# A routed two-block network on one core: marks and low halves on GpSimd, and another order around the routing

## What is computed

```python
x = _rmsnorm(hidden_states, ln_weight).reshape(-1, H)
logits = x @ router_weight
probs = jax.nn.softmax(logits, axis=-1)
top_vals, top_idx = jax.lax.top_k(probs, TOP_K)          # 4 of 16
aff = jnp.zeros((T, E)).at[jnp.arange(T)[:, None], top_idx].set(top_vals)
gu = jnp.einsum('th,ehi->eti', x, gate_up_proj)
gate, up = jnp.split(gu, 2, axis=-1)
expert_out = jnp.einsum('eti,eih->eth', jax.nn.silu(gate) * up, down_proj)
routed = jnp.einsum('te,eth->th', aff, expert_out)
shared = (jax.nn.silu(x @ shared_gate_w) * (x @ shared_up_w)) @ shared_down_w
return routed + shared
```

## Time and profile before

| | us |
|---|---|
| median of three runs | 1042.9 (1041.71 to 1045.14) |
| profiled execution: span from first to last instruction | 1041.2 |
| PE busy | 943.6 (91%) |
| DVE busy | 652.2 (63%) |
| ACT busy | 539.3 (52%) |
| POOL busy | 143.6 (14%) |

### The profile page before, as it was taken

The page is one execution under the profiler, slowest core; times in us unless marked ns, Lnnn a source line. Parts: engine busy times, 40 slices in busy tenths (PEclk is TensorE's granted clock), DMA queues, the critical chain, the costliest instruction groups (busy, mean ns, idle before and its releaser), DMA issues. The chain is left out here.

```text
span 1041.2 us, 21125 instructions
## 1 busy us (share of the span) xinstructions
PE 943.6 (91%) x7748; PEld 616.8 (59%) x7749; DVE 652.2 (63%) x1272; ACT 539.3 (52%) x857; POOL 143.6 (14%) x166
## 2 busy tenths in 40 slices
PE   5898988499999999999999999999999959975796
PEld 4444534267766666766776767677664438862453
DVE  5376786265666556566556665665666776677773
ACT  3655687155665545555556655654654213234674
POOL 0000000202102101210111210112016810002000
PEclk9989988799999999999999999999999979997999
DMA  8770633657885765776668776857887510000001
GB/s 290 247 234 1 232 131 132 199 159 240 263 263 182 244 194 189 242 260 195 217 213 255 228 252 211 252 201 233 260 240 230 162 47 1 1 0 1 1 21 61
DMA packets 164882, 181.76 MB, mean 175 GB/s; under 512 B 54609, under 2 KB 132433, under 8 KB 164850
## 3 DMA queue, kind: packets, MB, share of 16 engines
q1 hardware_dynamic: 152338, 147.35, 43.5%
q0 software_dynamic: 9808, 32.12, 9.7%
q10 hardware_dynamic: 2704, 1.87, 0.6%
HBM read 155.09 MB, written 14.68 MB: 163 GB/s over the span
## 5 line engine op out<-in xcount | busy, mean ns | idle before, releaser
L1083 DVE SCALAR_TENSOR_TENSOR w_lo<-raw_first,w_hi 128x1024 f16<-128x1024 f32 x144 | 172.6, 1223 | 82.4 <-ACT w_hi L577 80.6
L844 PE MATMUL pa<-x,w_hi 128*128 128x256 f16 (+2 forms) x576 | 172.5, 299 | 22.7 <-issue 13.3
L845 PE MATMUL pa<-x,w_hi 128*128 128x256 f16 (+2 forms) x576 | 172.3, 299 | 0.0
L846 PE MATMUL pa<-x,w_lo 128*128 128x256 f16 (+2 forms) x576 | 172.3, 299 | 0.0
L844 PE MATMUL pb<-x,w_hi 128*128 128x256 f16 (+2 forms) x576 | 170.9, 297 | 0.0
L845 PE MATMUL pb<-x,w_hi 128*128 128x256 f16 (+2 forms) x576 | 170.7, 296 | 0.0
L846 PE MATMUL pb<-x,w_lo 128*128 128x256 f16 (+2 forms) x576 | 170.6, 296 | 0.0
L577 ACT ACTIVATE w_hi<-raw_first 128x1024 f16<-128x1024 f32 x144 | 147.8, 1049 | 0.0
L585 ACT CAST early<-between 128x320 f16<-128x320 f32 (+1 forms) x144 | 68.4, 475 | 147.0 <-DVE between L1088 143.9
L1083 DVE SCALAR_TENSOR_TENSOR w_lo<-raw_last,w_hi 128x1024 f16<-128x1024 f32 x72 | 88.2, 1225 | 82.8 <-ACT w_hi L577 82.8
L1093 DVE TENSOR_TENSOR early<-between,early 128x320 f16<-128x320 f32 (+1 forms) x144 | 74.1, 515 | 74.8 <-ACT early L585 74.7
(11 more groups left out here) (272 smaller groups left out, 1621.2 us busy)
## 6 DMA issues: line engine op xcount, KB each, us to landing
raw_first<-in_gate_up SPq DMA_DIRECT2D x96, 512.0 KB, 4.8
raw_last<-in_gate_up SPq DMA_DIRECT2D x32, 512.0 KB
raw_first<-in_down SPq DMA_DIRECT2D x32, 512.0 KB, 4.3
raw_last<-in_down SPq DMA_DIRECT2D x32, 512.0 KB
chunks<-in_f SPq DMA_DIRECT2D x16, 704.0 KB, 5.9
slot_y<-chunks POOLq DMA_DIRECT2D x16, 512.0 KB, 3.2
chunks<-in_f SPq DMA_DIRECT2D x6, 768.0 KB, 4.6
raw_first<-in_sgate SPq DMA_DIRECT2D x6, 512.0 KB, 6.4
```

The costliest lines, as they stand in the source:

```text
L844: T.matmul(out, hi_a, hi_b, start=first, stop=False, **flags)
L845: T.matmul(out, hi_a, lo_b, start=False, stop=False, **flags)
L846: return T.matmul(out, lo_a, hi_b, start=False, stop=last, **flags)
L1083: V.scalar_tensor_tensor(w_lo[:, j % RING, c], raw[j % RING][:, c], W_SCALE, w_hi[:, j % RING, c], ALU.mult, ALU.subtract).then_inc(split_ ...
```

## The change

- POOL makes the tokens' low halves (`z_low` is gone from DVE's list and is POOL's first step for each tile), and the second half of the marks (`mark_places(nc.gpsimd, 1)`), behind the token stores. A new semaphore `found` releases it. `sum_lists` waits for one count from each engine.
- DVE's order changes: `hidden` of steps 4, 5, 6 moves ahead of `number`, `place` and the marks; the two low halves of piece 4 go ahead of `find_places`; the cast of `lists` goes ahead of the next unit's low halves. `hidden` in unit 0 waits explicitly for the `hidden_low` two steps earlier.
- ACT's order in unit 0 changes to match: `hi` before `make_ternary`, and `hidden_high` of steps 5 to 7 later.
- The first gather takes its numbers from `lists` directly, without the copy.
- `rows_in` becomes three semaphores: SP issues each turn as soon as its own gather has landed.
- PE reads `narrow` and branches first, and waits for `turned_in` inside either branch.

The diff, cut to its core (the semaphores' declarations and the two `tensor_copy`/`link` lines of `find_places` are left out):

```diff
+        def mark_places(engine, part):
+            for i in range(part * MARK, (part + 1) * MARK):
+                engine.tensor_scalar(at_row[:, i, :], place16[:, 0:P], at_f[:, 0, i:i + 1], None, ALU.is_equal)
+                ins = engine.tensor_scalar(at_col[:, i, :], place16[:, :], at_f[:, 1, i:i + 1],
+                                           token_ids[:, i // TOPK:i // TOPK + 1], ALU.is_equal, ALU.mult)
+            return ins
...
-                    sp.wait_ge(rows_in, U * (16 * len(ROUTED)))
-                    sp.nop(nofuse=True)
                     for j, w in enumerate(ROUTED):
+                        sp.wait_ge(rows_in[j], U * 16)
+                        sp.nop(nofuse=True)
                         turn_rows(j, rows16[0:w, j, :], w)
...
             for t in range(NT):
+                pool.wait_ge(z_hi_ready, t + 1)
+                nc.gpsimd.tensor_tensor(z16[:, t % Z_RING, 1, :], rows[:, t, :], z16[:, t % Z_RING, 0, :],
+                                        ALU.subtract).then_inc(z_ready, 1)
                 pool.wait_ge(z_ready, t + 1)
                 pool.dma_start(io["tokens"][t * P:(t + 1) * P, :],
...
+            pool.wait_ge(found, 1)
+            mark_places(nc.gpsimd, 1).then_inc(placed[1], 1)
...
             pool.wait_ge(listed, 1)
-            gather(0)
+            gather_rows(lists)
...
-                pe.wait_ge(placed, MARKS)
+                pe.wait_ge(placed[0], 1)
+                pe.wait_ge(placed[1], 1)
...
-                pe.wait_ge(turned_in, (u + 1) * (16 * len(ROUTED)))
                 few = pe.value_load(narrow[0:1, bass.ds(u, 1)], min_val=0, max_val=1)
                 with pe.If(few > 0):
+                    pe.wait_ge(turned_in, (u + 1) * (16 * len(ROUTED)))
+                    pe.nop(nofuse=True)
                     unit(u + 1, tiles_of(NARROW))
                 with pe.Else():
+                    pe.wait_ge(turned_in, (u + 1) * (16 * len(ROUTED)))
+                    pe.nop(nofuse=True)
                     unit(u + 1, ROUTED)
...
             lo(0, 3, 1)
+            hidden(0, 4, HALF, first_unit=True)
             number()
-            hidden(0, 4, HALF)
+            hidden_low(0, 4, HALF)
+            hidden(0, 5, HALF, first_unit=True)
             place()
-            hidden_low(0, 4, HALF)
-            z_low(6)
-            z_low(7)
             lo(0, 4, 0)
+            lo(0, 4, 1)
             find_places()
-            hidden(0, 5, HALF)
+            hidden(0, 6, HALF, first_unit=True)
+            hidden_low(0, 5, HALF)
             mark(0)
-            hidden_low(0, 5, HALF)
-            lo(0, 4, 1)
-            hidden(0, 6, HALF)
-            mark(1)
+            hidden(0, 7, HALF, first_unit=True)
             hidden_low(0, 6, HALF)
             lo(0, 5, 0)
-            hidden(0, 7, HALF)
             hidden_low(0, 7, HALF)
             lo(0, 5, 1)
-            lo(1, 0, 0)
-            lo(1, 0, 1)
             dve.wait_ge(list_summed, 1)
             V.tensor_copy(lists[:, :], list_ps).then_inc(listed, 1)
-            for j, half in HALVES[2:AHEAD]:
+            for j, half in HALVES[0:AHEAD]:
                 lo(1, j, half)
```

More of the change, by code:

```diff
@@ L290, in attention_and_experts @@
         listed = sem("listed")
-        placed = sem("placed")
+        found = sem("found")
+        placed = [sem("placed_dve"), sem("placed_pool")]
         list_summed = sem("list_summed")
         ids_ready = sem("ids_ready")
-        rows_in = sem("rows_in")
+        rows_in = [sem(f"rows_in{j}") for j in range(UNIT_COLS)]
         x_hi_ready = sem("x_hi_ready")
@@ L475, in _ @@
             pool.wait_ge(listed, 1)
-            gather(0)
+            gather_rows(lists)
             n = rounds_of(pool)
             with pool.Fori(0, n * EXPERTS) as u:
-                gather(u + 1)
+                gather_next(u)
                 store(u)
-            pool.wait_ge(rows_in, n * (EXPERTS * 48) + 48)
-            pool.nop(nofuse=True)
+            for j in range(UNIT_COLS):
+                pool.wait_ge(rows_in[j], n * (EXPERTS * 16) + 16)
+                pool.nop(nofuse=True)
             with pool.If(n < 2):
@@ L713, in _ @@
             silu(0, 5, HALF)
+            hi(0, 4, 1)
             make_ternary(6)
+            silu(0, 6, HALF)
             hidden_high(0, 5, HALF)
-            hi(0, 4, 1)
-            silu(0, 6, HALF)
+            hi(0, 5, 0)
             make_ternary(7)
+            silu(0, 7, HALF)
+            hi(0, 5, 1)
             hidden_high(0, 6, HALF)
-            hi(0, 5, 0)
-            silu(0, 7, HALF)
+            hidden_high(0, 7, HALF)
             make_ternary(8)
-            hidden_high(0, 7, HALF)
-            hi(0, 5, 1)
             make_ternary(9)
@@ L1084, in lo, with hidden @@
                                        ALU.mult, ALU.subtract).then_inc(split_ready, 1)
-            def hidden(U, m, n):
+            def hidden(U, m, n, first_unit=False):
                 dve.wait_ge(silu_ready, U * FH + m + 1)
+                if first_unit and m >= 2:
+                    dve.wait_ge(h_ready, m - 1)
                 V.scalar_tensor_tensor(hid[:, m % 2, 0:n], up_ps[m % 2][:, 0:n], 1.0 / W_SCALE, gated[:, m % 2, 0:n],
@@ L1094, in hidden_low @@
                                 ALU.subtract).then_inc(h_ready, 1)
-            def z_low(t):
-                dve.wait_ge(z_hi_ready, t + 1)
-                V.tensor_tensor(z16[:, t % Z_RING, 1, :], rows[:, t, :], z16[:, t % Z_RING, 0, :],
-                                ALU.subtract).then_inc(z_ready, 1)
             def choose():
@@ L1180, in find_places @@
                 link(V.tensor_scalar(at_int[:, 1, :], at_int[:, 1, :], P.bit_length() - 1, None, ALU.logical_shift_right))
-                link(V.tensor_copy(at_f[:, :, :], at_int[:, :, :]))
+                V.tensor_copy(at_f[:, :, :], at_int[:, :, :]).then_inc(found, 1)
+                dve.wait_ge(found, 1)
             def mark(part):
-                for i in range(part * MARK, (part + 1) * MARK):
-                    V.tensor_scalar(at_row[:, i, :], place16[:, 0:P], at_f[:, 0, i:i + 1], None, ALU.is_equal)
-                    ins = V.tensor_scalar(at_col[:, i, :], place16[:, :], at_f[:, 1, i:i + 1],
-                                          token_ids[:, i // TOPK:i // TOPK + 1], ALU.is_equal, ALU.mult)
-                ins.then_inc(placed, 1)
+                mark_places(V, part).then_inc(placed[0], 1)
             def add_shared():
@@ L1281, in _ @@
             lo(0, 1, 1)
-            hidden(0, 0, HALF)
-            z_low(0)
+            hidden(0, 0, HALF, first_unit=True)
             hidden_low(0, 0, HALF)
-            z_low(1)
             lo(0, 2, 0)
-            hidden(0, 1, HALF)
-            z_low(2)
+            hidden(0, 1, HALF, first_unit=True)
             hidden_low(0, 1, HALF)
-            z_low(3)
             lo(0, 2, 1)
-            hidden(0, 2, HALF)
+            hidden(0, 2, HALF, first_unit=True)
             choose()
```

20 lines of the change are left out of this document (10 added, 10 removed).

## The result

The changed kernel takes 1046.7 us (median of 20 runs, 1042.0 to 1050.1) against 1042.4 before (20 runs): a ratio of 1.0044, with a 95% interval of 1.0029 to 1.0058. That is 4.6 us slower, 3.0 to 6.0; I had forecast 16 us faster. Of the two terms one came as forecast and the other with the opposite sign and a larger size. Of the later run e5, one execution in six took 2856 us; its median is that of the other five.

What follows compares the result with a forecast made beforehand. PE bounds the kernel from 241 us on; the change can pay only between 109 and 200, in PE's waits and half-clock stretches. Gains of 5.4 + 10.8 = 16.2 us give 1026.7 us, range 1023 to 1030 (chance 0.43).

Steps and rivals of the forecast that it cites:

- Term 2: From E to the first routed matmul: earlier cast, split turns and early branch cut 23.85 us to 13.05, gaining 10.8.
- E: Start of the second `down` half behind the sum on PE: 175.78 us before, forecast at 170.4.
- Term 1: Unit 0: reordered DVE work and shared marks remove PE's waits, so E comes 5.4 us earlier.
- I take 0.70 a pair, near the rows of like width: GpSimd's half of the marks: 16 pairs at 0.70 us each, 11.2 us, plus 2.4 for disturbance.
- POOL idled 32.02 us there, which hides them: Tokens' low halves on POOL: eight subtractions at 0.93 us each, 15 us in all if doubled, hidden by POOL's idle time.
- the dear end, 1.41: Rival: GpSimd no quicker with narrow operations, 1.41 us per pair of marks, gain 5.7, 1037.2 us; chance 0.08.
- the slower case: Rival: GpSimd's pair dearer through fp16 and two scalars; above 1.71 us a pair slower than before, 1055.5 at 2.5; chance 0.06.
- The halves that take turns: Rival: DVE and GpSimd block each other for whole mark operations, both done after 17.65 us, 1030.8 us; chance 0.15.
- The branch's cost: Rival: PE's early branch does not help, code fetch paid again behind the rows, 2.6 us less gain, 1029.3; chance 0.08.

Runs made afterwards that it cites:

- e5: Changed kernel with GpSimd making 7 of 32 groups of marks and `hidden` 7 moved ahead of DVE's marks: 1029.4 us.
- e7: e6 with the token low halves of tiles 6 and 7 moved behind the marks on DVE: 1029.7 us.
- e8: Kernel before with 18 scalar operations, nine forms, added on GpSimd ahead of all other work to price them: 1045.8 us, one run.
- e11: e9 with PE waiting for the turned rows ahead of the load and the branch: 1034.3 us.
- e13: Changed kernel with DVE's tail (from `hidden_low` 6) waiting for GpSimd's marks: 1044.5 us.
- e3: Changed kernel with marks split unevenly, 6 of 32 groups on GpSimd and 26 on DVE: 1034.6 us.
- e1: Changed kernel with all marks on DVE, none on GpSimd: 1033.9 us.
- e6: e4 with `hidden` 7 moved ahead of the marks on DVE: 1032.1 us.
- e2: Kernel before with GpSimd making the second half of the marks as its only change: 1056.5 us.
- e4: e1 with the tokens' low halves back on DVE too: 1034.3 us.
- e9: e7 with DVE's low halves of the next unit's weights waiting until GpSimd has issued its first three gathers: 1028.9 us.
- e12: e9 with the cast of `lists` put back behind two low halves of the next unit's weights: 1030.0 us.
- e10: e9 with SP waiting for all three gathers before it turns rows: 1032.1 us.

## Why the prediction was wrong

**The bound was read rightly.** The change can only act between 109 and 200 us; from the first routed matmul to the end, the profiled executions of before and after differ by 1.0 us.

**Term 2 was right in size.** I forecast 10.8 us from E to the first routed matmul, and it was 10.3 (23.85 to 13.51). Most steps hold: the cast directly behind the sum, the first gather at E + 1.53 (forecast 1.6), the branch ended at E + 12.9 (12.85), and step 2 of the routed unit waited 1.63 us (1.8). That the branch ended on time is luck: it began at E + 9.0 in place of 8.2 and took 3.9 us in place of 4.65. One step was off without being felt, which is luck too: I had the last row at E + 10.3, and they came at E + 13.2, so the rows and not the branch came last, by little. The last turn began at E + 9.7 in place of 7.4. A code load of 16 KB (0.98 us) lies among the turns; that it delayed them is not shown. The clock fell behind the pause of 2.65 us nevertheless, which I had left open: the granted clock from 205.5 to 209.6 us was 0.60.

```profile
186.80:192.00 5.20, 5.19 (x33) 4.76 (x34) 0.00 (x0) 0.00 (x0) 0.00 (x0) 0.50 0.01 3
205.50:209.60 4.10, 4.10 (x19) 2.44 (x20) 0.00 (x0) 0.00 (x0) 2.72 (x4) 0.60 1.02 327
```

The first row is the sum, at half clock as forecast: 5.2 us for 2.78.

**Term 1 was wrong, by 18.6 us: E 13.15 late in place of 5.4 early.** The step that failed is "I take 0.70 a pair, near the rows of like width". What the 29.8 us of GpSimd's half hold beyond the forecast 13.6:

- the pair's price: (1.61 − 0.70) × 16 = 14.6;
- the operation held up by DVE's tail, 3.1, and the first wide one, 1.64 for 1.05, 0.6; the next four pairs, beside DVE's marks, took 1.66 to 1.74, and the first began 0.1 late, together 0.4;
- less the 2.4 that I had put in for disturbance by DVE's marks.

That is 16.3. Another 2.4 is in front of it: the places were found 2.4 us later than forecast because of `number`, which GpSimd's low halves stretched by 2.43. With the low halves back on DVE, out of the way of `number` and `place` (e7), the places are found 2.4 us earlier. There my step was "POOL idled 32.02 us there, which hides them": I asked what covers GpSimd's work, and not what it does to the engine beside it. The row was also the wrong one: the 32.02 us lie behind the last token store, and ahead of the last two stores GpSimd idled 11.94 us. With the 2.4 of `number` the wait for `hidden` 5 in unit 0 (2.2 us) is explained too, so the new order removed what it was to remove. The sum behind the marks took 0.2 less than I had put in.

**The bounds were the deeper fault.** The select, the iota and the scalar rows differ from a mark in width, and I let only width decide; the dear end, 1.41, was a multiply and add on 512 columns, and a compare on 195 with one on 128 costs more than that. So the truth lay outside both ends. The trace of before had no such compare on GpSimd; chances of 0.05 for a pair between 1.5 and 1.9 and of 0.06 for the slower case said more than I knew.

**The rivals.** "Slower" came true, but not by its reason: it put a dearer pair down to fp16 and two scalars, and by e8 it is the compare. The rival decides at marks at 181.1, and in the frame of before they came at 183.6 (59.1 behind the copy of the logits), 2.5 us above, with a pair of 1.61 that by itself lies below the 1.71 I gave; the lock's 3.1 and the 2.4 in front did the rest. By the prediction's own sum the price alone would not have made the kernel slower. The halves that take turns did not come: DVE's half beside GpSimd took 7.5 us against 6.45. The branch's cost was hidden as I had it, and e11 shows what it costs otherwise.

**The lock between the two engines.** Operations of DVE that read two tensors from SBUF and GpSimd's operations held each other up: 4.16 for 1.06 on a mark (gone in e13), 2.41 for 0.94 in `number`. Marks, with one tensor each, did so little (0.46 for 0.40 a pair in e3). The Trainium skill ("SBUF — State Buffer", Who interferes with whom) has just this distinction: two inputs from SBUF contend with GpSimd, one does not outside certain modes. By that rule the trace agrees on these rows, but for the 1.0 us that DVE's half still lost. The three operations of `number` with one tensor each, in fp32, were stretched as well, from 0.49 to 1.45 us. One tensor is thus not safe by itself; whether these ran in one of those modes no run here shows. I had read the page for the marks, where the runs show little of it, and not for the low halves, where they show 2.43 us.

## What to carry to other kernels

Bound the price of an operation on an engine by rows of the same operation, not the same width; where there is none, the range has to reach beyond the dearest neighbour. When work moves to an engine that shares something with its old one, list what the old engine does at that moment, and what the moved operation holds it up for. And when work is moved up a queue, follow what stands behind it on the other engines' queues: with `hidden` 7 behind the marks the next unit's weight loads went out some 14 us later (e1 against e6), and there they met the gathers.

## What the runs showed of the hardware

- On GpSimd a compare costs 1.5 to 2 times a multiply and add: 1.03 to 1.05 us with a multiply on 195 columns, whatever the types (one took 1.19), against 0.52 (fp16) and 0.68 (fp32).
- GpSimd's first operation behind a change of its configuration came 8.3 us after it, and 6.3 us after its input was there (e2). With 37 us of waiting behind the change it came without such a delay (changed kernel).
- DVE's operations with two tensors from SBUF lengthen a gather that GpSimd issues, and not only its arithmetic: the second gather took 1.83 to 1.85 us beside four low halves (changed kernel, e5, e6, e13) and 0.96 to 0.97 without (e1, e3, e4), the third 1.92 beside them (e9) and 0.92 behind them (e12). One first gather took 4.58 for 1.08 (e7); the low halves alone do not explain it.
- The branch into the expert's code took 3.4 to 7.2 us on PE (e10, e1), in each kernel only the first time (median of 24 in the changed kernel: 0.17).
